# Four-layer model on one core: slots stored by partition, skip products ahead of their wait, and a reordered end of the last layer

## The chip, the cores and the metric

One core of a Trainium2 chip runs the whole program as one launch. Its engines each work through their own list of instructions and meet only at semaphores: TensorE (PE) multiplies, VectorE (DVE), ScalarE (ACT) and GpSimd (POOL) do element work, SyncE (SP) issues DMAs. The metric is the device time of one execution in microseconds (us), of which several are taken; the host only transposes, pads and packs.

## The reference

The input is 8 sequences of 256 tokens with 128 features (2048 tokens). Four layers follow each other; each normalises x, computes a branch s from an attention-like block and a branch g from a feed-forward block, and adds s times silu(g) to x. Only the last layer is touched by the change. Its two branches:

```
# s: selective scan (256 channels, 16 states)
u, z = split(x @ W_in);  uc = silu(causal_conv(u) )
dt_r, B, C = split(uc @ W_x);  dt = softplus(dt_r @ W_dt + b_dt)
h[t] = exp(dt[t] * A) * h[t-1] + (dt[t] * u[t]) * B[t]
s = ((sum over the 16 states of h * C) + uc * D) * silu(z) @ W_out
# g: mixture of experts (8 experts, top 2, 256 slots each)
e1, e2 = top 2 of (x @ hash_kernel);  gates = softmax(their logits)
slot = running count of the expert's tokens; a token beyond 256 is dropped
g = sum over the two choices of gate * (gelu(x @ W1[e]) @ W2[e])
x = x + s * silu(g)
```

## The kernel before

Activations lie transposed: 128 features on the partitions, the 2048 tokens along the row, worked on in 4 chunks of 512 tokens (`NCH`) or in two halves of 1024 (four sequences each). Everything in the last layer is issued by the functions `l3_pe`, `l3_act`, `l3_dve`, `l3_pool` and `l3_sync`, one per engine; the order of each list is written out by hand, and many steps are hung on a slot number of the loop below.

**The scan loop.** There are 64 tiles, `TILES3`, in the order half, block of 128 channels, state: tiles 0 to 15 are half 0 and block 0, 16 to 31 half 0 and block 1, 32 to 63 the same for half 1. For tile i:

- SP fetches the B row of the state, spread over all partitions, from `b_dram` (`b_row`, L2143). It may run ahead until the buffer's previous user is done (four buffers).
- POOL makes `dbu` = du * B (L2107). It may run ahead too: tile i needs scan i-4 to be over.
- ACT makes exp(dt * A) in two PSUM banks (L1914). It waits for scan i-1, since there is one such buffer.
- DVE scans (L2028), then multiplies the previous tile's states by the C row (`weigh`, L2035).
- PE spreads the C row of the next tile by a product with a 0/1 matrix (`c_row`, L1662) and adds the weighed tile to y in PSUM by two products with the identity (L1771). On the first tile of a block the product of uc and diag(D) opens the sum (`skip`, L1668), at places 0, 16, 32 and 48.
- After each block DVE multiplies y by silu(z) (`gate_y`, L2041), two tiles into the next block.

**The experts** run inside this loop. POOL scatters every token row (128 features and the token's number, 129 words) to its slot in DRAM, `exp_in`, one indirect DMA for each of 16 token tiles and 2 choices (`dispatch`, L2066; 18 ahead of the loop, 14 in slots 0 to 13). Slot s is row s of `exp_in`. At `XE_SLOT + 2` SP loads both `exp_in` arrays back (L2168) and the token numbers by themselves into a small table, one word per row (L2169); POOL adds the two (L2128); PE transposes (`to_features`, L1675); ACT copies the result to SBUF (L1885). At slot 18 DVE turns the token numbers into row addresses `idx_g` (L2051, L2052). Each expert then takes four slots: up product (L1686), gelu on ACT with a table load before and behind it (L1888 to L1891), down product (L1696), four indirect DMAs on POOL to `exp_out` (`scatter`, L2097). At `MIX_SLOT + 7` SP gathers `exp_out` (L2178), and PE combines the two choices by products with diagonal gate matrices (`combine`, L1711; the diagonals are made by ACT, L1903 and L1904) in slots `MIX_SLOT` to `MIX_SLOT + 7`.

**Half 1's side work** in the loop: POOL finishes the step sizes dt and du of half 1 (L2114, L2118) in slots 13 to 20 and splits the B and C rows of half 1 into three bf16 parts (`split_rows`, L2078 to L2086) in slots 20 to 29. PE keeps fp32 accuracy in `c_row` that way.

**The end.** ACT loads the silu table and applies it to the first two chunks of g (L1927, L1931), then to the others (L1879). The projection with W_out (`project_out`, L1717) of half 0 is made in slots 52 and 53, that of half 1 behind the loop, after the last `gate_y`. `residual_dve` (L2191, L2193) multiplies s and g and adds them to x; chunks 0 and 1 are put between DVE's last tiles, chunks 2 and 3 stand last. SP stores each chunk of x when it is ready (L2250).

## Time and profile before

| | |
|---|---|
| three runs | 873.12, 878.82, 872.53 us |
| median | 873.12 us |
| profiled execution | 878.14 us, span 876.3 us |
| busy in the span | PE 83%, DVE 77%, ACT 57%, POOL 44% |
| mean granted TensorE clock | 0.91 |
| last layer's own work | about 568 to 876 us |
| scan loop, first scan to the last one's end | 613.95 to 860.41 us |

The span runs from the first to the last instruction on the core; the execution's time has 1.84 us more around it. Timeline rows give the start, the duration, the engine, the line and in brackets the idle time of the engine ahead of the row with the instruction that ended it. Durations of matmuls that follow each other overlap a little in the records, and one fp32 product of 512 columns shows as two records.

### The profile page before, as it was taken

The page shows a single profiled execution, that of the slowest core. Times are in us where ns is not written, and L with a number is a line of the kernel's source. Part 1 is how long each engine was busy: PE and PEld are TensorE (multiplying, and loading weights), DVE is VectorE, ACT ScalarE, POOL GpSimd, SP SyncE. Part 2 cuts the span into 40 slices and gives each one's busy share as a digit, 9 for nine tenths or more (in the row PEclk, how much of TensorE's full clock was granted, in tenths as well). Part 3 has the DMA queues.
Part 4 walks back from the last instruction along what each step waited for, and adds up shares of the span by engine and source line. Part 5 has one row for each costly group of instructions (what it writes and reads, how often), then busy time and mean ns, then how long its engine had stood idle before and what let it go on. Part 6 is the DMA issues. An engine that isn't in the chain of part 4 may idle for free.

```text
span 876.3 us, 13253 instructions
## 1 busy us (share of the span) xinstructions
PE 725.2 (83%) x4706; PEld 363.7 (42%) x4720; DVE 674.8 (77%) x1330; ACT 498.7 (57%) x726; POOL 381.2 (44%) x378
## 2 busy tenths in 40 slices
PE   6986886888878995878999989994875788878887
PEld 2333642433335772433444444441322344444444
DVE  3988378799845773687998933498897888989996
ACT  5796353777774552643666663558453364554464
POOL 0000205466653661510100000027997998999960
PEclk9997796899998995895999998987699899999999
DMA  9500000000025117300000000304538344545451
GB/s 358 237 1 0 4 0 1 1 20 31 21 77 157 44 39 235 90 1 1 3 2 2 3 1 1 120 15 149 171 134 215 121 161 161 179 163 190 140 169 48
DMA packets 41185, 75.97 MB, mean 87 GB/s; under 512 B 8431, under 2 KB 26296, under 8 KB 40096
## 3 DMA queue, kind: packets, MB, share of 16 engines
q1 hardware_dynamic: 36800, 67.41, 23.3%
q0 software_dynamic: 4320, 7.72, 2.7%
q8 instruction: 38, 0.62, 0.3%
q14 instruction: 27, 0.22, 0.1%
HBM read 59.28 MB, written 17.01 MB: 87 GB/s over the span
## 4 chain that ended last, share of the span: by engine, by line
PE 35%; DVE 28%; issue 14%; ACT 14%; POOL 4%; DMA 3%; SPq 1%; DVEq 0%; POOLq 0%; ACTq 0%
DVE arena L2028 5%; DVE band L2035 4%; DVE ttr_out L939 4%; DVE xq L939 3%; PE ps L749 3%; DVE arena L925 3%; POOL arena L2107 2%; PE ps L614 2%; PE ps L1367 2%; ACT ps L1914 2%; PE ps L295 2%; PE ps L727 2%; PE ps L708 1%; ACT arena L816 1%; DVE arena L908 1%
## 5 line engine op out<-in xcount | busy, mean ns | idle before, releaser
L2028 DVE TENSOR_TENSOR_SCAN arena<-ps,arena 128x1024 f32<-128x1024 f32 x64 | 146.6, 2291 | 22.0 <-ACT ps L1914 9.4
L816 ACT ACTIVATE arena<-ps 128x1024 f32<-128x1024 f32 x128 | 124.4, 1025 | 43.6 <-PE ps L738 27.0
L1914 ACT ACTIVATE ps<-arena,negA 128x1024 f32<-128x1024 f32 x64 | 71.5, 1117 | 101.3 <-DVE arena L2028 100.5
L1771 PE MATMUL ps<-band,w 128*128 128x512 f32 x256 | 122.7, 602 | 0.0
L925 DVE TENSOR_REDUCE arena<-ps 128x4 f32<-128x1024 f32 x64 | 76.1, 1218 | 12.2 <-PE ps L716 11.1
L2107 POOL TENSOR_TENSOR arena<-arena,gate 128x1024 f32<-128x1024 f32 x32 | 75.6, 2362 | 8.7 <-issue 5.7
L2035 DVE TENSOR_TENSOR band<-arena,ps 128x1024 f32<-128x1024 f32 x64 | 76.6, 1197 | 1.8 <-PE ps L1662 1.7
L993 POOL COPY arena<-arena 128x128 f32<-128x128 f32 x32 | 8.5, 295 | 158.1 <-PE ps L749 140.4
L2107 POOL TENSOR_TENSOR arena<-arena 128x1024 f32<-128x1024 f32 x32 | 75.1, 2363 | 4.1 <-DMA arena<-b_dram 2.4
L1662 PE MATMUL ps<-xq,sel 128*128 128x512 bf16 x115 | 36.6, 391 | 47.3 <-DVE band L2035 45.2
L749 PE MATMUL ps<-arena 128*32 128x256 f32 x1024 | 73.7, 409 | 1.3 <-ACT arena L816 1.2
L2066 POOL DMA_INDIRECT exp_in<-wf,wa x32 | 32.0, 999 | 95.3 <-DVE wa L1988 87.8
L1771 PEld LDWEIGHTS ps<-band,w 128*128 128x128 f32 x256 | 49.6, 194 | 42.8 <-issue 34.3
L727 PE MATMUL ps<-arena 32*128 32x256 f16 x512 | 51.5, 288 | 16.6 <-DVE arena L925 9.6
L716 PE MATMUL ps<-arena 32*128 32x256 f16 x512 | 53.0, 298 | 12.2 <-DVE arena L939 5.5
L1469 POOL DMA_INDIRECT e_out<-arena,band x39 | 37.8, 970 | 38.7 <-ACT arena L1418 25.0
L939 DVE CUSTOM_DVE_ANT_0 ttr_out<-ps,wf 128x256 bf16<-128x256 f32 x128 | 46.5, 420 | 7.7 <-issue 7.0
L939 DVE CUSTOM_DVE_ANT_0 xq<-ps,wf 128x256 bf16<-128x256 f32 x128 | 46.5, 420 | 6.7 <-issue 6.6
L952 POOL MEMSET arena<- 128x512 f16 x2 | 1.0, 524 | 102.8 <-DVE xT L2193 102.8
L1662 PEld LDWEIGHTS ps<-xq,sel 128*128 128x128 bf16 x128 | 8.3, 98 | 77.8 <-DVE band L2035 72.8
L749 PEld LDWEIGHTS ps<-arena 128*32 128x32 f32 x1024 | 27.9, 114 | 28.6 <-issue 14.6
L1300 POOL DMA_INDIRECT e_in<-arena,band x32 | 31.8, 992 | 10.2 <-issue 8.5
(385 smaller groups left out, 1661.4 us busy)
## 6 DMA issues: line engine op xcount, KB each, us to landing
gate<-b_dram SPq DMA_DIRECT2D x32, 512.0 KB, 3.9
arena<-b_dram SPq DMA_DIRECT2D x32, 512.0 KB, 4.4
wf<-pack1f_dram SPq DMA_DIRECT2D x1, 3076.0 KB, 14.5
wf<-bias_rows SPq DMA_DIRECT2D x1, 3072.0 KB, 15.7
exp_in<-band SPq DMA_DIRECT2D x2, 1032.0 KB, 18.6
exp_out<-band SPq DMA_DIRECT2D x2, 1024.0 KB, 20.5
e_in<-band SPq DMA_DIRECT2D x2, 1024.0 KB, 25.6
arena<-e_out SPq DMA_DIRECT2D x4, 512.0 KB, 5.8
```

The lines of the kernel that those rows point to most:

```text
L716: mm = pe.matmul(out_[:, a:a + SEQ], q_st[h, g, (b + 1) * SEQ + qb * P:(b + 1) * SEQ + (qb + 1) * P], k_st[h, g, (b + 1) * SEQ:(b + 2) * S ...
L727: mm = pe.matmul(out_[:, a:a + SEQ], k_st[h, g, b * SEQ + kb * P:b * SEQ + (kb + 1) * P], q_b[par][h, g, :], start=(l == 1 or kb == 0), st ...
L749: mm = pe.matmul(ps[32 * h:32 * h + 32, 6, (i // 2) * SEQ:(i // 2 + 1) * SEQ], v_b[pp][:, kb, i * HH + h, :], probs[i % 2][:, h, kb, :], s ...
L816: act.activation(probs[g % 2][:, 2 * pr:2 * pr + 2, :, :].rearrange("p h k n -> p (h k n)"), PAIRS[l][("S2", i, b)], ACT.Exp).then_inc(A[" ...
L925: dve.tensor_reduce(row_max[1 - par][:, :, g, 2 * pr:2 * pr + 2].rearrange("p b h -> p h b"), PAIRS[l][("S1", i, b)].rearrange("p (h b n) ...
L939: ins = dve.tensor_tensor_reduce(ttr_outs[unit % 2][:, n, :], PAIRS[l][("S1", i, b)][:, n * SEQ:(n + 1) * SEQ], bias_q[:, g * HH + h, WIN ...
L1662: mm = pe.matmul(ps[:, 6 + j, :], sel3[:, STATE + n, :], bc_parts[:, t0:t0 + CH], start=True, stop=True)
L1771: mm = pe.matmul(ps[:, j, :], ident, hc[i % 2][:, j * CH:(j + 1) * CH], start=False, stop=True, skip_group_check=True)
L1914: act.activation(dA_ps, dt3[:, cb, hf * HALF:(hf + 1) * HALF], ACT.Exp, scale=negA[:, cb * STATE + n:cb * STATE + n + 1]).then_inc(M["dA"], 1)
L2028: dve.tensor_tensor_scan(hst[i % 2], dA_ps, dbu[i % 4], 0.0, ALU.mult, ALU.add).then_inc(M["scan"], 1)
L2035: dve.tensor_tensor(hc[i % 2], hst[i % 2], pair(3), ALU.mult).then_inc(M["hc"], 1)
L2107: pool.tensor_tensor(dbu[i % 4], du[:, cb, hf * HALF:(hf + 1) * HALF], b_sb[i % 4], ALU.mult).then_inc(M["dbu"], 1)
```

## The change

1. **Slots by partition.** Slot s of an expert list is now row (s mod 128) * 16 + s div 128 of `exp_in`, and a token's number is coded in the same way, so that each partition's 16 rows lie side by side. A load is one contiguous piece per partition, and the token numbers come with the rows (a row in SBUF is now 129 words, so `s_sb` grows by 16 columns). The load is made in two halves, in slots 18 and 19 in place of 16; the four DMAs per load become two per half, and the sums and transposes follow in slots 17, 18 (POOL), 14, 15 (PE, two chunks each) and 17, 18 (ACT). The arithmetic of `idx_s` and of the number column has one more small instruction each, and `idx_g` is made in four instructions of 16 columns in place of two of 32. `exp_out` is read by partition too.
2. **Skip products ahead.** PE issues `skip` ahead of the wait for the first weighed tile of the block and of the next `c_row`.
3. **Half 1's side work.** The three copies of each split go to ACT (slots 15, 16, 23, 24); POOL keeps the two subtractions (slots 20, 21, 26, 27). The step sizes move to slots 22 to 33.
4. **Combination from tile 54** in place of 56, the half 0 projection from 51 in place of 52, the gather earlier in SP's list (slot 60 in place of 63), and the last expert's scatter in slot 55 in place of 56.
5. **Half 0's residuals** go from DVE to POOL, behind POOL's last tile.
6. **The end by quarters.** The first of the four half 1 projections stands in slot 61 behind a wait for the last scan, the second behind the loop; the last `gate_y` is made in two halves, each as soon as its half of y is there, and each is followed by its projection. ACT evicts the last two chunks of g behind its loop.

The start of the loop on PE. `arena,dD` is the skip product, `band` a weighed tile, `xq,sel` a C row, `arena,w` of L1597 the B and C projection. Before:

```order
L1662 MATMUL ps<-xq,sel 128x512 x2
L1597 MATMUL ps<-arena,w 64x512 x4
L1662 MATMUL ps<-xq,sel 128x512 x2
L1668 MATMUL ps<-arena,dD 128x512 x2
L1771 MATMUL ps<-band,w 128x512 x2
L1662 MATMUL ps<-xq,sel 128x512 x2
L1771 MATMUL ps<-band,w 128x512 x2
```

After the change:

```order
L1666 MATMUL ps<-xq,sel 128x512 x2
L1601 MATMUL ps<-arena,w 64x512 x4
L1672 MATMUL ps<-arena,dD 128x512 x2
L1666 MATMUL ps<-xq,sel 128x512 x2
L1780 MATMUL ps<-band,w 128x512 x2
L1666 MATMUL ps<-xq,sel 128x512 x2
L1780 MATMUL ps<-band,w 128x512 x2
```

The skip product moved ahead of the C row of tile 1, and so ahead of the wait for the first weighed tile.

POOL from slot 13. `exp_in` is the last dispatch, L2107 (L2146 after the change) makes a tile's `dbu`, L2114 and L2118 (L2153, L2157) are half 1's step sizes, L2128 (L2169) the sums, L2123 a subtraction of the split. Before:

```order
L2066 DMA exp_in<-wf,wa 2048x129
L2114 TENSOR_TENSOR arena<-arena 128x1024
L2107 TENSOR_TENSOR arena<-arena 128x1024 x2
L2118 TENSOR_TENSOR arena<-arena 128x1024
L2120 MEMSET arena 128x4
L2107 TENSOR_TENSOR arena<-arena,gate 128x1024
L2128 TENSOR_TENSOR wf<-wf,s_sb 128x512 x2
L2107 TENSOR_TENSOR arena<-arena,gate 128x1024
L2128 TENSOR_TENSOR wf<-wf,s_sb 128x512 x2
```

After the change:

```order
L2111 DMA exp_in<-wf,wa 2048x129
L2146 TENSOR_TENSOR arena<-arena 128x1024 x2
L2146 TENSOR_TENSOR arena<-arena,gate 128x1024 x2
L2169 TENSOR_TENSOR wf<-wf,s_sb 128x4x128 x2
L2146 TENSOR_TENSOR arena<-arena 128x1024
L2169 TENSOR_TENSOR wf<-wf,s_sb 128x4x128 x2
L2146 TENSOR_TENSOR arena<-arena 128x1024
L2146 TENSOR_TENSOR arena<-arena,gate 128x1024
L2123 TENSOR_TENSOR ttr_out<-sel,xq 32x512
L2146 TENSOR_TENSOR arena<-arena,gate 128x1024
L2123 TENSOR_TENSOR ttr_out<-sel,xq 32x512
L2146 TENSOR_TENSOR arena<-arena 128x1024
L2153 TENSOR_TENSOR arena<-arena 128x1024
```

The step sizes are behind the sums now, and the sums come one tile later, behind `dbu` of tile 17.

The end of PE's list. `dg` are combinations, `arena,w` the projection with W_out. Before, from `c_row` of tile 63:

```order
L1662 MATMUL ps<-xq,sel 128x512 x2
L1771 MATMUL ps<-band,w 128x512 x2
L1711 MATMUL ps<-dg,wf 128x128
L1711 MATMUL ps<-dg,s_sb 128x128
L1711 MATMUL ps<-dg,wf 128x128
L1711 MATMUL ps<-dg,s_sb 128x128
L1771 MATMUL ps<-band,w 128x512 x2
L1711 MATMUL ps<-dg,wf 128x128
L1711 MATMUL ps<-dg,s_sb 128x128
L1711 MATMUL ps<-dg,wf 128x128
L1711 MATMUL ps<-dg,s_sb 128x128
L1717 MATMUL ps<-arena,w 128x512 x4
```

After the change, from `c_row` of tile 62:

```order
L1666 MATMUL ps<-xq,sel 128x512 x2
L1780 MATMUL ps<-band,w 128x512 x2
L1715 MATMUL ps<-dg,wf 128x128
L1715 MATMUL ps<-dg,s_sb 128x128
L1715 MATMUL ps<-dg,wf 128x128
L1715 MATMUL ps<-dg,s_sb 128x128
L1726 MATMUL ps<-arena,w 128x512
L1666 MATMUL ps<-xq,sel 128x512 x2
L1780 MATMUL ps<-band,w 128x512 x4
L1726 MATMUL ps<-arena,w 128x512 x3
```

The last combinations stand two tiles earlier, but the first projection of half 1 now stands ahead of the last C row.

The core of the diff:

```diff
-        s_sb = sb("s_sb", [P, TOK])
+        s_sb = sb("s_sb", [P, TOK + NT])
-        XE_SLOT, UP_SLOT, UP_STEP, MIX_SLOT = 14, 18, 4, 56
+        XE_SLOT, UP_SLOT, UP_STEP, MIX_SLOT = 14, 18, 4, 54
-        OUT_SLOT = 52
+        OUT_SLOT = 51
...
+                if n == 0:
+                    if i:
+                        pe.wait_ge(M["yz"], i // STATE)
+                    skip(hf, cb)
                 pe.wait_ge(M["hc"], i + 1)
...
-                if n == 0:
-                    if i:
-                        pe.wait_ge(M["yz"], i // STATE)
-                    skip(hf, cb)
...
+                if i == NTL - 3:
+                    pe.wait_ge(M["scan"], NTL)
+                    part_out(2, 0)
+            part_out(3, 0)
             for c in range(2, NCH):
-                project_out(2 + c, c)
+                pe.wait_ge(M["yz"], 2 * NB + c - 2)
+                part_out(c, 1).then_inc(M["o_ps"], 1)
...
+            def split_mid(c):
+                act.wait_ge(M["pool_step"], c - 1)
+                act.activation(split_of(bc_mid2, c), split_of(bc_lo, c), ACT.Copy).then_inc(ROWS3["split"], 1)
+                act.wait_ge(*ROWS3.at("split", 2 * c - 1))
+                act.activation(chunk(bc_parts, c)[32:64, :], split_of(bc_mid2, c), ACT.Copy).then_inc(ROWS3["split"], 1)
...
                 if i == UP_SLOT:
-                    dve.wait_ge(M["xe_in"], 64)
-                    step(dve.tensor_scalar(slot, dest, 0.0, 2.0 * TOK, ALU.is_equal, ALU.mult))
-                    dve.scalar_tensor_tensor(idx_g, dest, -1.0, slot, ALU.add, ALU.add).then_inc(M["idx"], 1)
-            residual_dve(dve, 3, lambda c: chunk(o_half, c), lambda c: [(M["g_sb"], c + 1), ROWS3.at("o_sb", c + 1)], (0,))
+                    for h in range(2):
+                        dve.wait_ge(*ROWS3.at("xe_in%d" % h, 32))
+                    for k in range(2):
+                        ids = xe[k][:, :, P]
+                        step(dve.tensor_scalar(slot[:, k, :], ids, 0.0, 2.0 * TOK, ALU.is_equal, ALU.mult))
+                        ins = dve.scalar_tensor_tensor(idx_g[:, k, :], ids, -1.0, slot[:, k, :], ALU.add, ALU.add)
+                    ins.then_inc(M["idx"], 1)
             weigh(NTL - 1)
-            residual_dve(dve, 3, lambda c: chunk(o_half, c), lambda c: [(M["g_sb"], c + 1), ROWS3.at("o_sb", c + 1)], (1,))
-            gate_y(2 * NB - 1)
+            for j in range(2):
+                dve.wait_ge(M["y"], NTL + j)
+                last = chunk(sz[:, NB - 1, :], 2 + j)
+                dve.tensor_tensor(last, last, ps[:, j, :], ALU.mult).then_inc(M["yz"], 1)
...
-                if i in (13, 18):
+                if i in (22, 30):
...
-                elif i in (15, 20):
+                elif i in (24, 33):
...
-                if m == XE_SLOT + 2:
-                    sp_.wait_ge(M["scat"], 16 * 2 * NT)
+                if m in (18, 19):
+                    h = m - 18
+                    if h == 0:
+                        sp_.wait_ge(M["scat"], 16 * 2 * NT)
                     for k in range(2):
-                        rows = exp_in[k].rearrange("(t p) d -> p t d", p=P)
-                        sp_.dma_start(xe[k], rows[:, :, 0:P]).then_inc(M["xe_in"], 16)
-                        sp_.dma_start(r3k["dest"][:, k, :].unsqueeze(2), rows[:, :, P:ROW], allow_slow_non_contiguous=True).then_inc(M["xe_in"], 16)
+                        rows = exp_in[k].rearrange("(p t) d -> p t d", t=NT)
+                        part = slice(h * NT // 2, (h + 1) * NT // 2)
+                        sp_.dma_start(xe[k][:, part, :], rows[:, part, :]).then_inc(ROWS3["xe_in%d" % h], 16)
...
-                if m == MIX_SLOT + 7:
+                if m == MIX_SLOT + 6:
```

## Rows read from the trace of the kernel before

**Rows 1.** The page's costliest groups: busy, mean ns, idle before, its releaser.

```profile
L2028 DVE TENSOR_TENSOR_SCAN arena<-ps,arena 128x1024 f32<-128x1024 f32 x64 | 146.6, 2291 | 22.0 <-ACT ps L1914 9.4
L2035 DVE TENSOR_TENSOR band<-arena,ps 128x1024 f32<-128x1024 f32 x64 | 76.6, 1197 | 1.8 <-PE ps L1662 1.7
```

**Rows 2.** Timeline of DVE, early tiles of the loop.

```profile
628.44 1.22 DVE L2035 TENSOR_TENSOR band<-arena,ps 128x1024 f32<-128x1024 f32 x1 [1.44 <-PE ps L1662]
633.66 2.29 DVE L2028 TENSOR_TENSOR_SCAN arena<-ps,arena 128x1024 f32<-128x1024 f32 x1
637.19 2.29 DVE L2028 TENSOR_TENSOR_SCAN arena<-ps,arena 128x1024 f32<-128x1024 f32 x1
```

**Rows 3.** Timeline of PE, start of the loop.

```profile
614.84 3.65 PE L1597 MATMUL ps<-arena,w 128*64 128x512 f32 x4 [0.72 <-ACT arena L1801]
621.92 3.62 PE L1668 MATMUL ps<-arena,dD 128*128 128x512 f32 x4
```

**Rows 4.** Timeline of DVE, tiles 16 and 17 and the first gating.

```profile
676.49 2.29 DVE L2028 TENSOR_TENSOR_SCAN arena<-ps,arena 128x1024 f32<-128x1024 f32 x1 [4.10 <-POOL arena L2107]
681.25 2.29 DVE L2028 TENSOR_TENSOR_SCAN arena<-ps,arena 128x1024 f32<-128x1024 f32 x1 [1.35 <-POOL arena L2107]
684.43 1.22 DVE L2041 TENSOR_TENSOR arena<-arena,ps 128x1024 f32<-128x1024 f32 x1 [0.90 <-PE ps L1771]
```

**Rows 5.** Timeline of SP and POOL around the load of the slots.

```profile
660.11 0.37 SPq L2168 DMA_DIRECT2D wf<-exp_in  x1
667.39 3.73 SPq L2143 DMA_DIRECT2D gate<-b_dram  x2
...
657.90 0.99 POOL L2066 DMA_INDIRECT exp_in<-wf,wa  x1 [0.17 <-issue]
674.06 2.34 POOL L2107 TENSOR_TENSOR arena<-arena,gate 128x1024 f32<-128x1024 f32 x1 [5.70 <-issue]
676.36 2.49 POOL L2128 TENSOR_TENSOR wf<-wf,s_sb 128x512 f32<-128x512 f32 x2
```

**Rows 6.** Timeline of DVE and POOL: small table work of DVE, and POOL beside it.

```profile
582.56 0.18 DVE L1985 TENSOR_SCALAR wa<-wa 128x32 f32<-128x32 f32 x1
...
690.24 0.35 DVE L2051 TENSOR_SCALAR wa<-wa 128x32 f32<-128x32 f32 x1
690.62 2.28 DVE L2052 SCALAR_TENSOR_TENSOR wa<-wa 128x32 uint32<-128x32 f32 x1
...
690.50 2.35 POOL L2107 TENSOR_TENSOR arena<-arena,gate 128x1024 f32<-128x1024 f32 x1
698.41 1.15 POOL L2080 TENSOR_TENSOR ttr_out<-sel,xq 32x512 f32<-32x512 f32 x1
```

**Rows 7.** Timeline of DVE, the tile behind an expert's gelu.

```profile
708.31 2.29 DVE L2028 TENSOR_TENSOR_SCAN arena<-ps,arena 128x1024 f32<-128x1024 f32 x1 [1.31 <-ACT ps L1914]
```

**Rows 8.** The way to the gather: POOL, SP, and the tile's DMA landings.

```profile
824.65 1.01 POOL L2097 DMA_INDIRECT exp_out<-eo,wa  x1 [0.17 <-issue]
834.63 0.38 SPq L2178 DMA_DIRECT2D wf<-exp_out  x1
...
DMA to landing us min/median/max: 2.1/3.3/22.5
...
wf<-exp_out SPq DMA_DIRECT2D x4, 256.0 KB, 5.2
```

**Rows 9.** Timeline of DVE, ACT and PE at the end.

```profile
858.12 2.29 DVE L2028 TENSOR_TENSOR_SCAN arena<-ps,arena 128x1024 f32<-128x1024 f32 x1
873.09 0.69 DVE L2193 TENSOR_TENSOR xT<-xT,gate 128x512 f32<-128x512 f32 x1
...
861.27 0.39 ACT L1904 ACTIVATE dg<-w,wa 128x128 f32<-128x128 f32 x1
...
862.69 1.88 PE L1771 MATMUL ps<-band,w 128*128 128x512 f32 x4
868.59 3.67 PE L1717 MATMUL ps<-arena,w 128*128 128x512 f32 x8 [0.52 <-DVE arena L2041]
```

More of the change, by code:

```diff
@@ L1550, in build @@
         ew1_sb = wf[:, 0:E3 * HB3 * P]
-        xe = [t.rearrange("p (t d) -> p t d", d=P) for t in (wf[:, E3 * HB3 * P:E3 * HB3 * P + SLOTS], s_sb[:, :])]
+        halves_xe = (wf[:, E3 * HB3 * P:E3 * HB3 * P + NT * ROW], s_sb[:, :])
+        xe = [t.rearrange("p (t d) -> p t d", d=ROW) for t in halves_xe]
         xe_t = xn
@@ L1559, in build @@
         dg = [sb("dg%d" % i, [P, P])[:, :] for i in range(4)]
-        yk = xe
+        yk = [t[:, 0:TOK].rearrange("p (t d) -> p t d", d=P) for t in halves_xe]
         g_raw = xn
@@ L1719, in project_out, with part_out @@
                 mm.then_inc(M["o_ps"], 1)
+            def part_out(c, k):
+                return pe.matmul(ps[:, 2 + c, :], W3("W_out")[:, k * P:(k + 1) * P], chunk(sz[:, k, :], c),
+                                 start=(k == 0), stop=(k == NB - 1))
             def experts(i):
@@ L1863, in l3_act, with split_high @@
             act.wait_ge(M["idx"], 1)
+            def split_high(c):
+                act.wait_ge(M["dtr"], c + 1)
+                act.activation(chunk(bc_parts, c)[0:32, :], dtr_of(c)[0:32, :], ACT.Copy).then_inc(ROWS3["split"], 1)
+            def split_mid(c):
[3 more added lines that the diff above has]
+                act.activation(chunk(bc_parts, c)[32:64, :], split_of(bc_mid2, c), ACT.Copy).then_inc(ROWS3["split"], 1)
             def late_sizes(i):
+                if i in (15, 16):
+                    split_high(i - 13)
+                elif i in (23, 24):
+                    split_mid(i - 21)
                 if i < 2:
@@ L1881, in experts @@
             def experts(i):
-                if XE_SLOT + 2 <= i < XE_SLOT + 2 + NCH:
-                    c = i - XE_SLOT - 2
-                    act.wait_ge(M["xe_ps"], c + 1)
-                    act.activation(chunk(xe_t, c), ps[:, 2 + c % 2, :], ACT.Copy).then_inc(M["xe_t"], 1)
+                if XE_SLOT + 3 <= i < XE_SLOT + 3 + NCH // 2:
+                    for c in (2 * (i - XE_SLOT - 3), 2 * (i - XE_SLOT - 3) + 1):
+                        act.wait_ge(M["xe_ps"], c + 1)
+                        act.activation(chunk(xe_t, c), ps[:, 2 + c % 2, :], ACT.Copy).then_inc(M["xe_t"], 1)
                 e, at = (i - UP_SLOT) // UP_STEP, (i - UP_SLOT) % UP_STEP
@@ L1946, in l3_dve @@
             dve.memset(bc_parts[96:128, :], 0.0).then_inc(M["consts"], 1)
-            step(dve.tensor_copy(x_nat[:, :, P:ROW], W3("token").unsqueeze(2)))
+            first = W3("token")[:, 0:1].broadcast_to([P, NT])
+            step(dve.scalar_tensor_tensor(r31["m1"], first, 16.0 * P - 1.0, W3("token"), ALU.mult, ALU.add))
+            step(dve.tensor_scalar(x_nat[:, :, P], r31["m1"], 1.0 / P, 1.0 - NT, ALU.mult, ALU.add))
             dve.memset(dtr[0], 0.0)
@@ L1985, in l3_dve @@
             step(dve.tensor_scalar(ok, slot, float(CAP), None, ALU.is_le))
-            step(dve.tensor_scalar(slot, ok, -2.0 * SLOTS, 2.0 * SLOTS, ALU.mult, ALU.add))
+            step(dve.scalar_tensor_tensor(dest, slot, NT * P - 1.0, dest, ALU.mult, ALU.add))
+            step(dve.tensor_scalar(slot, slot, float(P), -P * (NT * P - 1.0), ALU.is_gt, ALU.mult))
             step(dve.tensor_tensor(slot, slot, dest, ALU.add))
-            dve.tensor_copy(idx_s, slot).then_inc(M["idx"], 1)
+            dve.tensor_scalar(idx_s, slot, 1.0 - NT * P, 1.0 / P, ALU.add, ALU.mult).then_inc(M["idx"], 1)
             taps(1, 0, 1)
@@ L2248, in _ @@
             for c in range(NCH):
-                sp_.wait_ge(x_ready, NCH * 3 + c + 1)
+                if c < NCH // 2:
+                    sp_.wait_ge(*ROWS3.at("x_half", c + 1))
+                else:
+                    sp_.wait_ge(x_ready, NCH * 3 + c - 1)
                 sp_.dma_start(chunk(out, c), chunk(xT, c)).then_inc(out_done, 16)
```

93 lines of the change are left out of this document (54 added, 39 removed).

## The prediction

> **What bounds the kernel now.** The change touches the last layer alone, so I read only that part of the trace, beginning with the page's costliest groups and then DVE's timeline. The two dearest DVE groups are the scan (64 times 2.291 us) and the weighing (64 times 1.197 us) [rows 1]. Two scans that follow each other without a disturbance start 3.53 us apart [rows 2], which is these two and a gap of 0.04. So the loop is bound by DVE: 64 times 3.53 is 226 us, and it took 246.5 us (613.95 to 860.41). The other 20 us are waits of DVE, three gatings and the table work; a change can win only these, and what lies behind the last scan. The reader should ask of each part of the change whether DVE waited for it. I find these places:
>
> - Tile 2's weighing waits 1.44 us for PE [rows 2], which had the skip product in front of the C row [rows 3].
> - Scans 16 and 17 wait 4.10 and 1.35 us for POOL's products, and the first gating 0.90 us for PE [rows 4].
> - The table work in slot 18 takes 0.35 and 2.28 us [rows 6].
> - Scans behind a gelu wait 1.31 us for ACT [rows 7]. This happens six times; two more hide behind a gating. Both table loads stay where they are, so these 7 us stay.
> - From the last scan's end (860.41) to the last residual's end (873.78) there are 13.4 us [rows 9].
>
> **Part 1, slots by partition.** Before, SP issues the four loads from 660.11 on and comes to B row 16 only at 667.39; POOL, which was done with tile 15, waits 5.70 us until 674.06 [rows 5]. Now B rows 16 and 17 stand ahead of the load. Each asks only for `dbu` of tile 12 and 13, the latter made right before the last dispatch at 657.90 [rows 5], so both are on their way by 658. POOL no longer has the two half 1 products in slots 13 and 15. It goes on at 658.9: four products at 2.3 us each end tile 17 at 668.2. The load starts at 660.1 as before (it waits for the last dispatch), and its first half is one piece of 4128 bytes per partition and array; I take it to be there by 668, 5.7 us after the last issue of it, as the wide loads of the gather [rows 8]. Two sums at 1.25 us [rows 5], tile 18 until 673.0, two sums, tile 19 until 677.9. DVE wants tile 16 at 671 and tile 19 at about 686, so both waits go: 5.45 us of idle time, less 0.13 us twice that every scan has ahead of it (637.19 in rows 2 against the weighing's end), gives **-5.2**. PE in slot 14 no longer stands at the sums, so the first gating finds its y: **-0.9**. The transposes in pairs and ACT's pairs of copies (two of 0.6 us, in the 2.4 us that the period of 3.53 leaves beside an exponential of 1.1) are hidden; without that cover they would cost under 2 us.
>
> The table work is where this part pays. Before, DVE's one-input operation took 0.35 us, while its like took 0.18 with POOL idle; the two-input one took 2.28 us and ended with POOL's product, 690.50 + 2.35 [rows 6]. Both were held up by a POOL operation, and POOL's next one got in between them. Now there are four operations, and by my schedule DVE comes to them at 682.8, when POOL has a full queue: the end of tile 21 (1.0 us), a subtraction (1.15 [rows 6]), tile 22 (2.36) and the step size that was moved to slot 22 (2.37). If each operation waits for one of these, the four take 6.9 us; then tile 23 must wait for scan 19, and POOL is out of work. If the one-input ones slip through, as a strided input might let them, it is the end of tile 21, the subtraction and little else: 2.3 us. A full tile product in place of the subtraction would give 8.1. I take 6.9, since the one row of such an operation, 0.35 against 0.18, speaks for waiting. Against 2.55 before: **+4.35**, with bounds -0.3 and +5.6.
>
> The Trainium skill ("SBUF — State Buffer", Who interferes with whom) has the rule behind this: DVE and GpSimd share a port pair under an exclusive lock, a DVE instruction with two SBUF inputs contends with one of GpSimd that reads SBUF, and a `tensor_scalar` in a two-port mode does too. The rows of the table work agree. By the Trainium skill ("VectorE: DVE Perf Modes", Mode 2×_2P) a strided SBUF input with an even outer size may still run in that mode, which no row here shows. It speaks for the dearer end.
>
> The extra small operations ahead of the loop: one in front of the routing's results, on which PE waits, one behind, under DVE's later slack of 2 us. At 0.18 us [rows 6] and the step behind it: **+0.2**, between 0 and 0.45.
>
> **Part 2, skip ahead.** PE ended the B and C projection at 618.49 and stood idle until the C row; then came the skip product with 3.62 us [rows 3]. That is 1.2 GHz, since the same shape takes 1.88 later [rows 9], at 2.4 GHz. Ahead of the wait it runs from 618.5 to 622.1. C row 1 follows at once, y of tile 0 by 625.5 and C row 2 by 626.5, while DVE asks for it at 627.0: **-1.4**; at worst, with the low clock going on, half of it. At tiles 16, 32 and 48 DVE did not wait for PE because of it: 0.
>
> **Part 3, side work of half 1.** The copies on ACT are 0.6 us each (its other copies of 512 columns), at most two a slot and one eviction of 0.4, in the window of 2.4 us. The gelu slots 22, 26 and so on are not touched. Should two copies and their meeting overrun, each of slots 23 and 24 would cost under 1 us. POOL between slots 28 and 33 has six products, eight scatters of 1.27 us and a step size, 26.7 us, and begins some 12 us ahead of a DVE that takes 18.9: no wait. Taken as 0.
>
> **Part 4, combination from 54.** Nothing on DVE's path waits for it now, so it wins nothing by itself, but it frees PE's end. It has a margin: the last scatters moved ahead from 824.65 [rows 8] by one product, to 822.3, and end at 827.2 with a landing by 830; the gather's first pair lands 5.2 us after its issue [rows 8], at 835.5. PE wants it at 835.5, DVE would notice at 837. 0, and thin.
>
> **Parts 5 and 6, the end.** I count from the last scan's end S. DVE weighs tile 62 until S+1.1. ACT's diagonals stand behind the silu table and two silus, as before; the last ended at 861.66, which is S+1.25 [rows 9]. So PE's last combination ends at S+1.8, the first projection (0.92 us, a quarter of 3.67 [rows 9]) at S+2.6, C row 63 at S+3.0. The weighing of tile 63 ends at S+4.3 (before: S+3.7). The y products, 0.86 us each [rows 9], end at S+5.6 and 6.5; the gating halves at 6.4 and 7.3 (0.7 each); three projections at 7.4, 8.3 and 9.2; four residual operations of 0.69 [rows 9] from 8.4 to 11.2. Before it was S+13.4: **-2.2**. If the diagonals were not in the way it would be -3.5; if every meeting costs 0.1 more, -1.2. POOL's four half 0 operations (1.25 us each by the sums) run from about S to S+5 beside DVE operations with one input in PSUM, and end 3 us before DVE's own.
>
> **Sum.** -5.2 - 0.9 + 4.35 + 0.2 - 1.4 - 2.2 = -5.15 us. The profiled execution took 878.14 us and would take 873.0. It is 5 us above the median of the three runs, of which two agree within 0.6 us. I take the difference from the median: 873.12 - 5.1 gives **868.0 us**.
>
> **The rivals.**
> 1. DVE's table work does not wait in a chain: the one-input operations pass, or POOL happens to stand at its limit of tiles ahead. For it: the input is strided, as no row shows; POOL's position is my estimate. Against it: the 0.35. It gives 2.3 in place of 6.9 us, 863.4 us.
> 2. The gain of part 1 goes in part into a new wait: the first half of the load lands late (one of the old ones took 9 us), POOL stands at its sums in slot 17 with tile 18 behind them. From 676 on each us late is one on DVE. With some 3 us, 871 us.
> 3. Slower than before: the gather's first pair comes too late for slot 54, PE stands there with C row 56 behind it, and ACT's diagonals too. Above 837 (on the old clock) each us late is a us on the loop; the gain is gone at 842, and it is 1% slower at 851. The scatters landed after 3.3 us, but once after 22.5 [rows 8]: with that, gather at 848.5, pair at 854, 885 us. Against it: the median.
> 4. The skip product isn't ready in time or the low clock lasts: 0.7 us only, in the range.
>
> **How the numbers follow.** About 1% (8.7 us) can be told from no change. The forecast 0.50 (its own range 865 to 870); rival 1 0.28 (862 to 865.5); rival 2 0.17 (869.5 to 874); rival 3 0.05. Faster by over 1%, below 864.4, is most of rival 1 and a little of the forecast: 0.27. Slower by over 1% is 0.03 of rival 3. Same: 0.70. The range goes from 862 to 872: rival 1 entire, the forecast and half of rival 2, with the runs' own spread of about 1 us in it.
>
> **What would show it.** Scans 16 and 17 without idle time; tile 2's weighing without its 1.44; the four table operations at near 7 us together, each ending with a POOL operation; six scans with 1.31 us still; the last scan to the last residual about 11 us, with PE's projection ahead of C row 63; the loop about 243.3 us. It is wrong if the table work is short, if POOL waits for DMA in slot 17, or if PE waits for the gather.

## The result, and the profile after

| | before | after |
|---|---|---|
| median of 9 runs each | 875.76 us | 868.69 us |
| lowest and highest | 869.28 to 878.82 | 863.56 to 870.19 |
| profiled execution, its span | 878.14, 876.3 us | 863.56, 861.8 us |

The ratio of the runs is 0.9903, with a 95% interval of 0.9877 to 0.9928: 8.5 us less, between 6.3 and 10.8 (the two medians differ by 7.1). The change is faster, but by 0.97%, and the 1% that the prediction sets as the limit for "faster" lies inside the interval. The two profiled executions differ by 14.6 us, but 4.3 of them lie ahead of the last layer, where no line differs (experiment 12). So I compare stages of the last layer, not spans. They are taken from DVE's timeline in each profile: head is from the end of the last normalised chunk (L242) to the first scan, loop from there to the last scan's end, end from there to the last residual's end.

```
profile                  normalised at   head    loop     end   last layer
before                       567.76     46.19  246.46   13.37     306.02
after                        563.46     45.56  238.89   11.30     295.75
```

On the page of the changed kernel (columns as in rows 1) the scan's idle time is 16.9 us in place of 22.0, and POOL, which ended 5.7 us of it before, no longer ends any; ACT's 9.7 us, nearly all of them behind the gelus, are all that the profile names:

```profile
L2061 DVE TENSOR_TENSOR_SCAN arena<-ps,arena 128x1024 f32<-128x1024 f32 x64 | 146.6, 2291 | 16.9 <-ACT ps L1944 9.7
L2068 DVE TENSOR_TENSOR band<-arena,ps 128x1024 f32<-128x1024 f32 x64 | 76.5, 1196 | 2.3 <-PE ps L1666 2.3
```

DVE's timeline of the changed kernel at tiles 16 to 19 (start, duration, line; scans are counted from 0) answers to [rows 4] and to the table work of [rows 6]:

```profile
665.71 2.29 DVE L2061 TENSOR_TENSOR_SCAN arena<-ps,arena 128x1024 f32<-128x1024 f32 x1
669.24 2.29 DVE L2061 TENSOR_TENSOR_SCAN arena<-ps,arena 128x1024 f32<-128x1024 f32 x1
671.52 1.22 DVE L2074 TENSOR_TENSOR arena<-arena,ps 128x1024 f32<-128x1024 f32 x1
674.01 2.29 DVE L2061 TENSOR_TENSOR_SCAN arena<-ps,arena 128x1024 f32<-128x1024 f32 x1
...
677.33 1.53 DVE L2087 TENSOR_SCALAR wa<-wf 128x16 f32<-128x16 f32 x1
678.89 0.18 DVE L2088 SCALAR_TENSOR_TENSOR wa<-wf,wa 128x16 uint32<-128x16 f32 x1
678.99 1.12 DVE L2087 TENSOR_SCALAR wa<-s_sb 128x16 f32<-128x16 f32 x1
680.15 0.18 DVE L2088 SCALAR_TENSOR_TENSOR wa<-s_sb,wa 128x16 uint32<-128x16 f32 x1
680.26 2.29 DVE L2061 TENSOR_TENSOR_SCAN arena<-ps,arena 128x1024 f32<-128x1024 f32 x1
```

Scans 16 and 17 start 3.53 us after each other without a wait, the gating follows at once, and the two-input table operations take 0.18 us each. POOL beside them:

```profile
676.48 2.35 POOL L2146 TENSOR_TENSOR arena<-arena,gate 128x1024 f32<-128x1024 f32 x1
678.91 1.18 POOL L2123 TENSOR_TENSOR ttr_out<-sel,xq 32x512 f32<-32x512 f32 x1
680.16 2.37 POOL L2146 TENSOR_TENSOR arena<-arena 128x1024 f32<-128x1024 f32 x1
```

The first one-input operation ended 0.03 us behind tile 21's product (678.83), the second 0.02 us behind the subtraction. The subtraction started 0.08 us after the product's end, and the two-input operation (678.89) was in before it.

The end, on PE and DVE, answers to [rows 9]; the last scan ends at 847.91:

```profile
849.77 1.02 PE L1726 MATMUL ps<-arena,w 128*128 128x512 f32 x2
850.63 0.59 PE L1666 MATMUL ps<-xq,sel 128*128 128x512 bf16 x2
851.06 3.60 PE L1780 MATMUL ps<-band,w 128*128 128x512 f32 x8
854.49 2.74 PE L1726 MATMUL ps<-arena,w 128*128 128x512 f32 x6
...
851.32 1.22 DVE L2068 TENSOR_TENSOR band<-arena,ps 128x1024 f32<-128x1024 f32 x1 [2.29 <-PE ps L1666]
858.52 0.69 DVE L2101 TENSOR_TENSOR xT<-xT,gate 128x512 f32<-128x512 f32 x1
```

### The profile page after: what moved, and what is told of

The parts are those of the page before. It is cut to its first block, busy times and chain, and to the rows that moved or that the text cites. A ratio compares the mean times of both kernels' runs of the same rounds, so it can differ in the third digit from the quotient of the medians.

```text
span 861.8 us, 13274 instructions
## 1 busy us (share of the span) xinstructions
PE 717.6 (83%) x4720; PEld 357.5 (41%) x4720; DVE 672.2 (78%) x1331; ACT 502.1 (58%) x732; POOL 383.1 (44%) x376
## 4 chain that ended last, share of the span: by engine, by line
DVE 33%; PE 32%; issue 15%; ACT 13%; DMA 4%; POOL 2%; SPq 1%; DVEq 0%; POOLq 0%; ACTq 0%
DVE band L2068 5%; DVE arena L2061 5%; DVE ttr_out L939 4%; DVE xq L939 4%; PE ps L749 3%; DVE arena L925 3%; PE ps L295 2%; PE ps L1367 2%; DVE arena L908 1%; PE ps L727 1%; POOL arena L2146 1%; PE ps L708 1%; ACT ps L1944 1%; ACT arena L816 1%; PE ps L614 1%
## 5 line engine op out<-in xcount | busy, mean ns | idle before, releaser
L2061 DVE TENSOR_TENSOR_SCAN arena<-ps,arena 128x1024 f32<-128x1024 f32 x64 | 146.6, 2291 | 16.9 <-ACT ps L1944 9.7
L925 DVE TENSOR_REDUCE arena<-ps 128x4 f32<-128x1024 f32 x64 | 76.0, 1218 | 12.2 <-PE ps L716 11.2
L2146 POOL TENSOR_TENSOR arena<-arena,gate 128x1024 f32<-128x1024 f32 x32 | 75.4, 2361 | 5.1 <-DMA gate<-b_dram 3.0
L2146 POOL TENSOR_TENSOR arena<-arena 128x1024 f32<-128x1024 f32 x32 | 75.1, 2362 | 1.7 <-DVE arena L2061 1.2
L1666 PE MATMUL ps<-xq,sel 128*128 128x512 bf16 x128 | 39.0, 387 | 42.0 <-DVE band L2068 40.1
L749 PE MATMUL ps<-arena 128*32 128x256 f32 x1024 | 71.8, 400 | 1.3 <-ACT arena L816 1.2
```

Source lines behind the costliest of these rows:

```text
L749: mm = pe.matmul(ps[32 * h:32 * h + 32, 6, (i // 2) * SEQ:(i // 2 + 1) * SEQ], v_b[pp][:, kb, i * HH + h, :], probs[i % 2][:, h, kb, :], s ...
L925: dve.tensor_reduce(row_max[1 - par][:, :, g, 2 * pr:2 * pr + 2].rearrange("p b h -> p h b"), PAIRS[l][("S1", i, b)].rearrange("p (h b n) ...
L1666: mm = pe.matmul(ps[:, 6 + j, :], sel3[:, STATE + n, :], bc_parts[:, t0:t0 + CH], start=True, stop=True)
L2061: dve.tensor_tensor_scan(hst[i % 2], dA_ps, dbu[i % 4], 0.0, ALU.mult, ALU.add).then_inc(M["scan"], 1)
L2146: pool.tensor_tensor(dbu[i % 4], du[:, cb, hf * HALF:(hf + 1) * HALF], b_sb[i % 4], ALU.mult).then_inc(M["dbu"], 1)
```

## The experiments

Where nothing else is said, an experiment is the changed kernel with one edit. The figures in "extra" are by how much the distance from the scan before to this scan exceeds the regular 3.53 us; a gating alone makes 1.23, a gelu 1.17. Experiments 6 and 11 were run several times. The others are one execution each, whose whole time says little, so they are compared by stages: in the four whose edits concern the end (6 to 9) the loop took 238.85 to 238.89 us, beside the changed kernel's 238.89, and in the two profiles of the kernel before 246.46 and 246.73.

```
profile            normalised at   head    loop     end   extra of scans 4, 5 | 16, 17, 18 | 19
before                 567.76     46.19  246.46   13.37   1.55 0.34 | 3.96 1.22 2.13 | 2.55
after                  563.46     45.56  238.89   11.30   0    0    | 0    0    1.23 | 2.71
1 skip back            567.27     46.34  243.80   11.30   1.47 0.34 | 0    0    1.23 | 5.46
2 table in slot 20     562.32     45.56  243.18   11.31   0    0    | 0    0    1.22 | 0 (scan 21: 7.06)
3 sizes back           567.26     46.33  244.51   11.29   0    0    | 0    0    2.98 | 6.39
4 load in slot 16      564.43     45.54  238.99   11.30   0    0    | 0    0.42 1.24 | 2.43
5 old layout           566.23     46.18  237.95   11.30   0    0    | 0    0    1.22 | 1.07
6 diagonals first      567.04     46.34  238.87   10.13   0    0    | 0    0    1.23 | 2.71
7 residuals on DVE     568.60     46.30  238.85   11.30   0    0    | 0    0    1.22 | 2.70
8 combination at 56    566.43     45.54  238.89   13.08   0    0    | 0    0    1.23 | 2.75
9 one last gating      568.40     46.38  238.86   12.47   0    0    | 0    0    1.22 | 2.71
10 old layout, slot 16 567.31     46.22  243.14   11.30   0    0    | 1.27 3.79 1.24 | 1.17
11 both improvements   566.84     46.34  237.51   10.13   0    0    | 0    0    1.23 | 0 (scan 23: 2.57)
12 before again        564.47     45.13  246.73   13.37   0.33 0.33 | 5.46 1.21 2.16 | 2.53
```

**1. The skip product back behind the C row.**

```diff
-                if n == 0:
-                    ...
-                    skip(hf, cb)
                 pe.wait_ge(M["hc"], i + 1)
...
                     c_row(*TILES3[i + 1][0:2])
+                if n == 0:
+                    ...
+                    skip(hf, cb)
```

> The changed kernel with the skip products back behind the C row; nothing else is different. Theory: the skip product in front of C row 2 was what tile 2's weighing waited for, so about 1.4 to 1.9 us of idle time of DVE come back in tiles 2 and 3 and the loop (first scan to the last one's end, 238.9 us in the changed kernel) takes about 240.6. Rival: the wait came from the low granted clock at the loop's start, which the changed kernel's profile shows high; then, with a high clock, the skip product back in its old place costs under 0.5 us.

Scans 4 and 5 lost 1.81 us, as the theory says. But this profile had the low clock too, so I ask the others: PE's skip product took 1.98 us in the changed kernel's profile and 2.65 in experiment 6's, and in neither did the weighing wait. Here it is in the old place:

```profile
620.76 1.03 PE L1666 MATMUL ps<-xq,sel 128*128 128x512 bf16 x2 [2.61 <-DVE band L2068]
621.58 3.62 PE L1672 MATMUL ps<-arena,dD 128*128 128x512 f32 x4
```

and in the new one, in experiment 6, after a projection at the same low clock:

```profile
614.28 3.65 PE L1601 MATMUL ps<-arena,w 128*64 128x512 f32 x4 [0.72 <-ACT arena L1815]
617.85 2.65 PE L1672 MATMUL ps<-arena,dD 128*128 128x512 f32 x4
```

In both profiles the projection ran at the low clock. Directly behind it the skip product took 2.65 us, so it ran in part at the high clock; behind the 2.61 us in which PE waits for DVE it took 3.62, all of it at the low one. From 613 to 635 us the mean granted clock was 0.86 in experiment 6 and 0.70 here.

The rival holds in part: experiment 12, the kernel before with the clock higher there, lost only 0.66 us at scans 4 and 5. The new place makes the wait vanish at either clock; what it is worth depends on the clock. The surprise is scan 19, 2.75 us dearer. DVE came to its table work 1.8 us later relative to POOL, and met other POOL operations:

```profile
683.74 1.01 DVE L2087 TENSOR_SCALAR wa<-wf 128x16 f32<-128x16 f32 x1
684.78 0.18 DVE L2088 SCALAR_TENSOR_TENSOR wa<-wf,wa 128x16 uint32<-128x16 f32 x1
684.88 2.32 DVE L2087 TENSOR_SCALAR wa<-s_sb 128x16 f32<-128x16 f32 x1
687.23 2.27 DVE L2088 SCALAR_TENSOR_TENSOR wa<-s_sb,wa 128x16 uint32<-128x16 f32 x1
```

**2. The table work in slot 20.**

```diff
-                if i == UP_SLOT:
+                if i == UP_SLOT + 2:
                     for h in range(2):
```

> The changed kernel with DVE's four table operations in slot 20 in place of slot 18. In the changed kernel POOL's work of 128x1024 goes on there without a meeting between two operations (tile 24's product and a step size, back to back), while in slot 18 each of POOL's operations stood behind a wait for its own previous one. Theory: a two-input DVE operation that comes up behind a one-input one is locked out only if POOL's next operation is already in its queue with nothing to wait for; so here the four take about 4.9 us in place of 3.0. Rival: the short two-input operations of 16 columns are not locked out at all, only the one-input ones wait for what is running: at most 2.7 us.

Scan 21 came 7.06 us late. The rival's 2.7 us are out. The theory's kind of wait is what is seen, but its number was too low by one POOL operation, as DVE arrived while the step size of slot 22 was still running. DVE, then POOL:

```profile
683.25 0.44 DVE L2087 TENSOR_SCALAR wa<-wf 128x16 f32<-128x16 f32 x1
683.73 2.27 DVE L2088 SCALAR_TENSOR_TENSOR wa<-wf,wa 128x16 uint32<-128x16 f32 x1
685.92 2.37 DVE L2087 TENSOR_SCALAR wa<-s_sb 128x16 f32<-128x16 f32 x1
688.33 2.27 DVE L2088 SCALAR_TENSOR_TENSOR wa<-s_sb,wa 128x16 uint32<-128x16 f32 x1
```

```profile
681.30 2.36 POOL L2153 TENSOR_TENSOR arena<-arena 128x1024 f32<-128x1024 f32 x1
683.61 2.35 POOL L2146 TENSOR_TENSOR arena<-arena 128x1024 f32<-128x1024 f32 x1
685.92 2.34 POOL L2146 TENSOR_TENSOR arena<-arena,gate 128x1024 f32<-128x1024 f32 x1
688.22 2.34 POOL L2157 TENSOR_TENSOR arena<-arena 128x1024 f32<-128x1024 f32 x1
```

Each of DVE's four ends with one of POOL's four, and POOL's start with no gap, since none of them waits for the one ahead.

**3. The step sizes of half 1 back in POOL's slots 13, 15, 18, 20.**

```diff
-                if i in (22, 30):
+                if i in (13, 18):
...
-                elif i in (24, 33):
+                elif i in (15, 20):
```

(the counts waited for follow)

> The changed kernel with half 1's step sizes on GpSimd back in slots 13, 15, 18 and 20. Theory: the stall at tiles 16 and 17 came from the B rows that stood behind the load of the slots, so with the B rows ahead of it the two extra products of 2.36 us in slots 13 and 15 only use up POOL's lead: scan 16 does not wait, tile 17's product ends at about the time at which the scan wants it, and the loop loses under 1.5 us. Rival: POOL's work was as much of the cause as the B rows; then scans 16 to 19 wait some 3 to 5 us in all, and the loop takes 242 to 244 us.

The loop took 5.6 us more. My theory was wrong in size, and the rival came close to the number (244.5 against its 242 to 244) with another mechanism: scans 16 and 17 waited 0.06 us at most beyond the regular gap, but POOL's second pair of sums came late and PE stood 3.04 us at the transposes. The gating waited 1.75 us, and the weighing of tile 17 another 3.30, since C row 17 had the transposes and, by part 2, the skip product in front of it:

```profile
678.07 1.22 DVE L2074 TENSOR_TENSOR arena<-arena,ps 128x1024 f32<-128x1024 f32 x1 [1.75 <-PE ps L1780]
686.14 1.22 DVE L2068 TENSOR_TENSOR band<-arena,ps 128x1024 f32<-128x1024 f32 x1 [3.30 <-PE ps L1666]
```

```profile
681.08 2.34 PE L1679 MATMUL ps<-w,wf 128*128 128x128 f32 x8 [3.04 <-POOL wf L2169]
683.21 2.41 PE L1672 MATMUL ps<-arena,dD 128*128 128x512 f32 x4
685.45 0.59 PE L1666 MATMUL ps<-xq,sel 128*128 128x512 bf16 x2
```

The move of the step sizes, which the prediction counted as nothing for itself, is what keeps this away. What the wait would be with the sizes back and the skip product behind the C row, no run shows.

**4. The load in slots 16 and 17, new layout.**

```diff
-                if m in (18, 19):
-                    h = m - 18
+                if m in (16, 17):
+                    h = m - 16
...
-                if i in (XE_SLOT + 3, XE_SLOT + 4):
+                if i in (XE_SLOT + 2, XE_SLOT + 3):
```

> The changed kernel with the load of the slots back in SP's slots 16 and 17 and POOL's sums in slots 16 and 17; the slots lie by partition. Theory (place): B row 16 is again issued only behind the load, 2 us after the last dispatch's landing, so tile 16's product starts about 8 us late and scan 16 waits 1 to 3 us; the place was worth that much. Rival (layout): the old wait came from the issue of four loads in small pieces (7.3 us on SP); two loads take 0.8 us, B row 16 is on its way at 658 and no scan waits: the loop takes 238.9 us as in the changed kernel.

POOL did wait 3.76 us for B row 16, but it had the lead for it; scan 17 waited 0.42 us and the loop was 0.1 us longer. The rival holds nearly whole.

**5. The old layout, load in slots 18 and 19.**

```diff
-                        rows = exp_in[k].rearrange("(p t) d -> p t d", t=NT)
-                        sp_.dma_start(xe[k][:, part, :], rows[:, part, :])
+                        rows = exp_in[k].rearrange("(t p) d -> p t d", p=P)
+                        sp_.dma_start(xe[k][:, part, :], rows[:, part, 0:P])
+                        sp_.dma_start(r3k["dest"][:, k, part].unsqueeze(2), rows[:, part, P:ROW])
```

(and the numbering, the table work in two operations, and the reading of `exp_out` as before the change)

> The changed kernel with the old layout of the slots: row s is slot s, the load is made in 512-byte pieces with the token numbers by themselves, in two halves of four DMAs, in the new places; the table work is in two operations again. Theory (place alone suffices): B rows 16 and 17 are ahead of the load, so scans 16 and 17 don't wait; B rows 18 and 19 come late by the 7 us that the issue of the pieces takes, and scans 18 or 19 wait up to 2 us. Rival: the slow load holds back POOL's sums in slot 17 and with them tile 18, and scans 18 and 19 wait 4 us or more, as scans 16 and 17 did before the change: the layout is what counts.

POOL waited 0.71 and 2.46 us for the slow loads, and none of scans 16 to 18 waited. For the stall at tiles 16 and 17 the place alone suffices. The loop was even 0.9 us shorter than the changed kernel's, since the table work in two operations cost 1.07 us in place of 2.71. But the slow load took lead from POOL: its product of tile 22 began 5.8 us before the scan of that tile, against 10.7 in the changed kernel, and behind the moved step sizes and four scatters the product of tile 37 came late. Scan 37 lost 1.10 us by that (1.09 in experiment 10, nothing in the changed kernel):

```profile
751.45 2.29 DVE L2058 TENSOR_TENSOR_SCAN arena<-ps,arena 128x1024 f32<-128x1024 f32 x1 [1.23 <-POOL arena L2140]
```

**10. The old layout, load in slots 16 and 17** (experiment 5 with the edit of 4).

> The kernel with the old layout, now with its load in slots 16 and 17 and the sums in slots 16 and 17, half 1's step sizes in the late slots; it fills the fourth corner beside the changed kernel, the one with the load in slot 16 and the one with the old layout in slot 18, whose loops took 238.9, 239.0 and 238.0 us. Theory: either the place or the layout suffices, so with neither the B rows 16 and 17 stand behind some 4 to 7 us of small-piece issues, and scans 16 to 18 wait 2 to 6 us in all. Rival: POOL's freed slots 13 and 15 alone removed the wait, and the loop takes 238 to 239 us here too.

Scans 16 and 17 waited again, 5.06 us together against 5.18 before the change:

```profile
671.48 2.29 DVE L2058 TENSOR_TENSOR_SCAN arena<-ps,arena 128x1024 f32<-128x1024 f32 x1 [1.40 <-POOL arena L2140]
678.81 2.29 DVE L2058 TENSOR_TENSOR_SCAN arena<-ps,arena 128x1024 f32<-128x1024 f32 x1 [3.93 <-POOL arena L2140]
```

With 4 and 5 this makes a square: extra of scans 16 and 17 is 0 (new layout, slot 18), 0.42 (new, 16), 0 (old, 18) and 5.06 us (old, 16). For these two scans each of the two does the work of both. In all four the step sizes stand in the late slots, so their move alone does not remove the wait.

**6. The last diagonals ahead of ACT's silu table.**

```diff
                 if i == NTL - 1:
+                    experts(i)
                     act.preload_act_table_set("silu_and_others")
```

> The changed kernel with ACT's last four diagonals ahead of the table load and the two silus in slot 63. In the changed kernel PE's last combinations wait for them, then the first half 1 projection and C row 63 follow, and tile 63's weighing waits 2.3 us for that. Theory: with the diagonals 2.4 us earlier, the projection runs right behind the last scan and C row 63 follows the weighing of tile 62 within 0.1 us; the weighing waits under 0.8 us, and the end (last scan's end to the last residual's end) goes from 11.3 to about 9.8 us. Rival: the first projection, which waits for the last scan, is what holds C row 63; then nothing changes. Whole time: 1.5 us less than the changed kernel, hardly to be told in the runs.

The weighing of tile 63 waited 1.12 in place of 2.29 us, and the end fell to 10.13, a little over the theory's 9.8. In the runs (ratio 0.990, 0.9871 to 0.9928) these 1.2 us don't show against the changed kernel's 0.9903. What remains of the wait is the first projection, which still ends 0.6 us behind DVE's weighing of tile 62, and C row 63 itself.

**7. Half 0's residuals back on DVE.**

```diff
+            ... the two operations on chunk 0
             weigh(NTL - 1)
+            ... the two operations on chunk 1
```

> The changed kernel with half 0's residuals back on DVE, one pair before and one behind the weighing of tile 63. Theory: DVE's 2.9 us lie in its wait for PE's C row 63 (2.3 us) and in the one for the y products (1.3 us), so the end grows by under 0.5 us and the move to POOL was worth about nothing. Rival: the second pair comes when y is ready and the end grows by 1.4 us.

The end is 11.30 us, to the hundredth as in the changed kernel. Part 5 was worth nothing on this path.

**8. Combination from 56, half 0's projection from 52.**

```diff
-        XE_SLOT, UP_SLOT, UP_STEP, MIX_SLOT = 14, 18, 4, 54
+        XE_SLOT, UP_SLOT, UP_STEP, MIX_SLOT = 14, 18, 4, 56
...
-                if i == NTL - 3:
+                if i == NTL - 1:
```

> The changed kernel with the combinations and half 0's projection back two tiles and one tile later (56 and 52). The first half 1 projection must then stand behind the loop's last tile, and ACT's last two evictions one slot later, or the engines would wait for each other in a circle. Theory: the combinations of four token tiles with their diagonals come behind the last scan again, the last of them ahead of the projections, and the end (11.3 us in the changed kernel) takes 12.5 to 14 us: the earlier combination is what makes the new end short. Rival: the end is short because of the halves, and it takes 11.3 to 11.8 us here too.

13.08 us, inside the theory's 12.5 to 14: the combinations of six token tiles ran between the last scan's end and the projections, four more than in the changed kernel. The halves and the rest without the earlier combination would have won 0.3 us of the old 13.37.

**9. One last gating, projections behind it** (the end of before, with all else as changed).

> The changed kernel with one gating of the last block in place of two halves, and all four half 1 projections behind it, as before the change; combinations and residuals stay where the change put them. Theory: C row 63 no longer has a projection in front of it (0.9 us less wait of tile 63's weighing), but four products of 0.9 us and the longer gating come behind y: the end takes 12 to 12.6 us against 11.3. Rival: PE has the same work either way and its end does not move: 11.3 us.

12.47 us. With the halves and the early projection undone the end grows by 1.17 us, with the earlier combination undone (experiment 8) by 1.78. Together that is more than the 2.07 us won, so the two overlap and neither number is a share of it.

**11. Both improvements:** experiment 6 and the table work in slot 22, behind which the next scan waits for a gelu anyway.

```diff
-                if i == UP_SLOT:
+                if i == UP_SLOT + 4:
```

> The changed kernel with ACT's last diagonals ahead of the silu table, and with DVE's four table operations in slot 22, where the next scan waits 1.3 us for ACT's gelu in any case. Theory: POOL has run to its limit of tiles ahead there, so at most one of its products stands in the way, and the table work costs under 1 us in place of 2.7; with the end's 1.2 us the last layer takes about 3 us less than in the changed kernel (292 to 293 us from its normalised input to the last residual, against 295.8). Rival: the operations wait for POOL one after the other as in slot 20 (7 us), and the loop takes 243 us. Ratio to the kernel before: 0.987 by the theory.

Ratio to the kernel before 0.9843 (0.9814 to 0.9872), median 867.28 us beside 878.87 for the kernel before on the same chip. The last layer took 293.98 us. Three table operations are short, the last took 2.22 us behind a POOL product; with 2.57 - 1.17 = 1.40 us in place of 2.71 the slot hides half of it, less than I expected. It is the fastest version of this study by its ratio. Its interval lies below that of the changed kernel (from 0.9877) by only 0.0005, and the two were measured beside different runs of the kernel before; the stages, 293.98 against 295.75 us, say the same.

**12. The kernel before, profiled again.**

> The kernel before, profiled once more. The profiled execution of the kernel before reached the end of the last layer's normalisation at 567.8 us, that of the changed kernel at 563.5, though no line ahead of it differs; eight other profiles of variants lie between 562.3 and 568.6. Theory: this is a spread between executions that has nothing to do with the change, and the last layer itself is steady: from its normalised input to the last residual 306 us within 1 us here too, wherever the point lies. Rival: the last layer's time moves from run to run by several us as well, and the 10.3 us between the two first profiles are partly chance.

The last layer took 305.2 us (306.0 in the first profile), while the point at which it begins moved by 3.3 us. Over all fourteen profiles that point lies between 562.3 and 568.6, whatever the kernel. Within the layer the two profiles of this kernel differ in an instructive way: scans 4 and 5 lost 1.2 us less, scan 16 lost 1.5 us more. Counted from the normalised input, DVE came to scan 16 2.3 us sooner, of which 1.07 lie in the head, while POOL's product of tile 16 began only 0.8 us sooner (at 669.98 here, at 674.06 in the first profile). The rest was waited away at scan 16. From this I take it that in the kernel before part 2 alone would have been worth little or nothing; no run has it alone.

## Why the prediction came out as it did

The time, 868.69 us, lies 0.7 us from the forecast of 868.0, and this closeness is mostly luck, since two errors met: I subtracted 5.1 us from the median of three runs, 873.12, and the median of nine is 875.76, 2.6 more; and the change gave 7.1 us by the medians, 1.9 more than forecast. By the ratio it gave 8.5 us and by the stages 9.6 (with the head counted as 0), so the forecast of 5.15 lies outside the measured 6.3 to 10.8. Most of what is missing is one term, the table work. Term by term, from the table:

- **Tiles 16 and 17, -5.2:** measured -5.18. The schedule was right to the operation; in the changed kernel POOL ran dispatch, four products, two sums without a pause. But the forecast spoke of the B rows' place and of the layout as one thing. Either suffices (experiments 4, 5, 10); and it did not price the moved step sizes, without which 5.6 us come back (experiment 3; the skip product's new place takes part in that).
- **First gating, -0.9:** measured -0.90.
- **Table work, +4.35:** this is the term that failed. It measured +0.16, near the bound of -0.3, the case of rival 1, though not for its reason. The strided one-input operations do wait for POOL: 1.53 and 1.12 us, each up to an end of a POOL operation. What I had wrong was that each of the four would wait for a POOL operation of its own. The two-input ones got in between. They do so when POOL's next operation waits for the one ahead and leaves a gap of 0.08 us, and don't when the next is free to go. DVE's table work in all fourteen profiles agrees with this: a two-input operation recorded 0.06 to 0.08 us behind POOL's end took 0.18 or 0.19 us where POOL's next one had a gap of 0.06 to 0.08 us, and waited for it in full, 2.27 to 2.29 us, where POOL's next one had none (the kernel before, experiment 2, the last operation of experiment 1). In experiment 2 all four waited, 7.06 us, and in experiments 1 and 3 some. The forecast's 6.9 us was the price of the neighbouring case, and DVE 1.8 us later would have met most of it (5.46).
- **Skip product, -1.4:** measured -1.89, as scan 5's 0.34 went too. By experiment 12 it counts only because the stall at tile 16 is gone.
- **Side work of half 1, 0:** near enough. The old 0.16 at scan 33 is gone, but scan 25 came 0.35 us late, and not because of the copies: ACT's exponential for it began right behind scan 24 and ended at 702.55 as it should, POOL's product had ended at 694.30, and the profile shows nothing that DVE waited for in the last 0.4 us. The profiler names ACT only as the last to release it. Experiments 5 and 10 have the same 0.36 us at scan 26. The cause stays open.

```profile
702.99 2.29 DVE L2061 TENSOR_TENSOR_SCAN arena<-ps,arena 128x1024 f32<-128x1024 f32 x1 [0.48 <-ACT ps L1944]
701.43 1.12 ACT L1944 ACTIVATE ps<-arena,negA 128x1024 f32<-128x1024 f32 x1 [0.69 <-DVE arena L2061]
```

- **Combination from 54, 0:** right that nothing waits for the gather; but it carries the end: without it the end is 13.08 us.
- **End, -2.2:** measured -2.07. The forecast's order of events is the profile's: diagonals, combinations, projection, C row 63, weighing. S+4.3 for the weighing's end was S+4.63, and 11.2 for all was 11.30.
- **Operations in the head, +0.2:** the head depends more on the clock than on this. The granted clock fell there in two ways. In nine profiles it was 0.83 in each of the first two stretches of 10 us behind the normalised input: the old numbering took 46.18 to 46.22 us, the new 46.30 to 46.38, +0.14. In four with the new numbering it was 0.66 and then 1.00: 45.54 to 45.56 us, and in experiment 12 with the old 45.13, +0.42. Both lie inside the bounds of 0 and 0.45.

Rivals 2 and 3 didn't come. The sums' load was never late, and POOL waited 2.98 us for B row 60 behind the gather in the changed kernel without reaching DVE. The Trainium skill's rule on the shared port pair ("SBUF — State Buffer", Who interferes with whom) fits these profiles. The strided one-input operations were held up too (1.53 and 1.12 us), as the mode in the Trainium skill ("VectorE: DVE Perf Modes", Mode 2×_2P) allows. That each of four in a row would be held up was the step that I added.

## What to carry to other kernels

A gain ahead of a stall that has another cause is worth nothing until the stall is gone, so order the terms by place and ask of each where it would be waited away. Where two edits remove the same wait, undo each alone and both together: a square of four runs told here what no one of them could. And small DVE operations beside a busy GpSimd have a price that is not theirs: 2.4 to 7.1 us of delay for the same four instructions (experiments 4 and 2), by the moment at which they come. Make them fewer (two cost 1.07 us in experiment 5), or put them where DVE waits anyhow (1.4 us in experiment 11).

## What the runs showed of the hardware

- A DVE operation of 128x16 or 128x32 took 0.16 to 0.19 us where GpSimd did not hold it up, and up to 2.37 us where it did; those ended 0.02 to 0.05 us behind a GpSimd operation's end in each of the profiles. This held for one SBUF input, contiguous (128x32) or strided (128x16), and for two. Twice (experiments 3 and 11) a one-input operation recorded 0.01 to 0.02 us behind the start of a GpSimd operation that followed a memset still passed, in 0.16 and 0.17 us.
- GpSimd operations that don't wait for each other follow without a gap; a wait for the own previous one leaves 0.08 us. That gap decided whether a DVE operation that came 0.06 to 0.08 us behind the end got in.
- The granted clock of TensorE at the start of the loop (613 to 635 us) was 0.69 and 0.92 in two profiles of the same kernel, 1.00 in the changed one's. The same skip product took 3.62, 2.65 and 1.98 us in different profiles, so a term that rests on PE's speed there has a spread of over 1 us between executions.
